# Score matmuls of attention units 4 to 15 issued in eight groups of four instead of twenty smaller groups

## The reference

```python
qkv = x @ attn_qkvw + attn_qkvb                      # (2, 512, 3, 32, 32)
scores = jnp.einsum('bhqd,bhkd->bhqk', q, k) * scale
probs = jax.nn.softmax(scores, axis=-1)
ctx = jnp.einsum('bhqk,bhkd->bhqd', probs, v)
```

## Time and profile before

| | us |
|---|---|
| median of 3 runs | 728.29 |
| lowest and highest | 725.28, 728.97 |
| the profiled execution | 726.08 |
| its span | 724.3 |
| TensorE busy | 705.1 |
| VectorE busy | 472.0 |
| ScalarE busy | 425.9 |

### The profile page before, as it was taken

The page is one execution under the profiler, slowest core; times in us unless marked ns, Lnnn a source line. Parts: engine busy times, 40 slices in busy tenths (PEclk is TensorE's granted clock), DMA queues, the critical chain, the costliest instruction groups (busy, mean ns, idle before and its releaser), DMA issues.

```text
span 724.3 us, 11766 instructions
## 1 busy us (share of the span) xinstructions
PE 705.1 (97%) x3477; PEld 527.6 (73%) x3484; DVE 472.0 (65%) x831; ACT 425.9 (59%) x919; POOL 280.0 (39%) x206
## 2 busy tenths in 40 slices
PE   6999999999999999999999999999999998999996
PEld 5778668668677686686776776857767776888884
DVE  5887567466575584574675755567678798765564
ACT  4458668677686685686766866863655682311111
POOL 5573250170162152143134158735734834211111
PEclk9999999999999999999999999999999999999999
DMA  8667436426436336335444377827733421331101
GB/s 287 177 189 222 115 83 197 122 75 210 109 84 196 92 104 193 92 109 148 134 118 103 92 229 197 257 90 231 249 107 126 155 80 60 129 103 58 59 29 59
DMA packets 55732, 98.97 MB, mean 137 GB/s; under 512 B 10896, under 2 KB 21392, under 8 KB 54800
## 3 DMA queue, kind: packets, MB, share of 16 engines
q1 hardware_dynamic: 55408, 98.13, 44.6%
q10 hardware_dynamic: 288, 0.39, 0.2%
HBM read 56.41 MB, written 16.65 MB: 101 GB/s over the span
## 4 chain that ended last, share of the span: by engine, by line
PE 71%; issue 15%; DVE 6%; POOL 3%; ACT 3%; SPq 1%; DMA 1%; POOLq 0%; DVEq 0%; ACTq 0%
PE bank L469 43%; PE bank L595 8%; PE bank L565 8%; PE bank L609 8%; POOL xb L1205 2%; PE bank L720 1%; PE bank L521 1%; DVE st L1459 1%; DMA w_raw<-in_wqkv 1%; DVE quant L1491 1%; POOL mv L1186 1%; DVE wb_lo L1517 1%; DVE x1s L1506 1%; SPq L232 1%; SPq L227 1%
## 5 line engine op out<-in xcount | busy, mean ns | idle before, releaser
L863 ACT ACTIVATE probs<-bank 128x512 f32<-128x512 f32 x256 | 152.3, 598 | 117.9 <-PE bank L595 115.0
L1385 DVE TENSOR_REDUCE m_col<-bank 128x1 f32<-128x512 f32 x256 | 172.7, 687 | 74.9 <-PE bank L565 74.2
L868 ACT ACTIVATE bank<-bank,m_col 128x512 f32<-128x512 f32 x256 | 169.4, 662 | 19.6 <-DVE m_col L1385 18.0
L469 PE MATMUL bank<-big_hi,w_hi 128*128 128x512 f32 x384 | 157.0, 409 | 5.8 <-DVE big_lo L1280 5.5
L469 PE MATMUL bank<-big_lo,w_hi 128*128 128x512 f32 x384 | 152.7, 398 | 0.0
L469 PE MATMUL bank<-big_hi,w_lo 128*128 128x512 f32 x384 | 151.4, 394 | 0.0
L565 PE MATMUL bank<-kp,qp 96*128 96x512 f32 x256 | 101.5, 397 | 0.7 <-ACT bank L868 0.7
L595 PE MATMUL bank<-qp,kp 98*128 98x512 f32 x256 | 101.0, 398 | 0.0
L469 PEld LDWEIGHTS bank<-big_hi,w_hi 128*128 128x128 f32 x384 | 73.4, 191 | 25.0 <-DVE big_lo L1280 5.9
L469 PEld LDWEIGHTS bank<-big_hi,w_lo 128*128 128x128 f32 x384 | 73.0, 190 | 17.1
L469 PEld LDWEIGHTS bank<-big_lo,w_hi 128*128 128x128 f32 x384 | 73.7, 192 | 14.8
(11 more groups left out here) (139 smaller groups left out, 1106.5 us busy)
## 6 DMA issues: line engine op xcount, KB each, us to landing
w_raw<-in_wqkv SPq DMA_DIRECT2D x7, 1536.0 KB, 7.3
c_raw<-in_ctx SPq DMA_DIRECT2D x16, 512.0 KB, 4.0
qp<-q_hi SPq DMA_DIRECT2D x128, 64.0 KB, 2.0
kp<-k_hi SPq DMA_DIRECT2D x124, 64.0 KB, 2.0
big_raw<-in_xT SPq DMA_DIRECT2D x16, 256.0 KB, 6.0
qp<-q_lo SPq DMA_DIRECT2D x64, 64.0 KB, 2.0
c_scratch<-c_q SPq DMA_DIRECT2D x16, 256.0 KB, 2.2
r_all<-r_scratch SPq DMA_DIRECT2D x64, 64.0 KB, 2.0
```

What stands on the lines that cost most here:

```text
L469: mm = nc.tensor.matmul(dst, lhs[a], rhs[b], start=(k == 0 and n == 0) if first is None else False, stop=(k == last_k and n == 2))
L863: nc.scalar.activation(probs[:, j, t, :], bank(ST0 + i % 2), ACT.Exp).then_inc(sem["exp_ok"], 1)
L868: nc.scalar.activation(bank(max_bank(s, n)), bank(max_bank(s, n)), ACT.Exp, bias=m_col[:, n:n + 1], accum_out=l_col[:, 1 - par, n:n + 1]). ...
L1385: nc.vector.reduce_max(m_col[:, n:n + 1], bank(max_bank(s, n)), AX, negate=True).then_inc(sem["rowmax"], 1)
```

## The change

For steps from 4 on, both slot functions give the same slot for n and n+1 with n even: 2, 7, 12, 18, 23, 29, 34, 40. At such a place S n, T n, S n+1, T n+1 are issued. Only the even ones wait: S n for X n-2, T n for E n-1, which covers the odd ones behind them. On ScalarE the order at a place becomes E n, X n, E n+1, X n+1. Steps 16 and 17 project nothing and keep their order.

```diff
+        def by_pairs(s):
+
+            return not isinstance(s, int) or s >= 4
+
+        def score_slot(n, s):
+
+            if by_pairs(s):
+                return 2 + 38 * (n // 2) // 7
+            return 6 + (34 * n + 14) // 15 if s == 1 else 2 + (38 * n + 14) // 15
+
+        def transposed_slot(n, s):
+
+            if by_pairs(s):
+                return 2 + 38 * (n // 2) // 7
+            return 8 + (39 * n + 14) // 15 if s == 2 else 2 + 3 * n
...
                     if n >= 2 and isinstance(s, int) and s == UNITS:
                         pe.wait_ge(sem["sum_ok"], NS * (s - 1) + n - 1)
+                    elif by_pairs(s) and n >= 2:
+                        if n % 2 == 0:
+                            pe.wait_ge(sem["sum_ok"], NS * (s - 1) + n - 1)
                     elif n >= 3:
...
-                    if n >= 2:
+                    if n >= 2 and not (proj and by_pairs(s)):
                         pe.wait_ge(sem["exp_ok"], NS * (s - 2) + n - 1)
+                    elif n >= 2 and n % 2 == 0:
+                        pe.wait_ge(sem["exp_ok"], NS * (s - 2) + n)
...
-                    if maxima and done < NS and q == score_slot(done, second):
-                        score(done)
-                        done += 1
+                    for _ in range(2):
+                        if maxima and done < NS and q == score_slot(done, s):
+                            score(done)
+                            done += 1
+                        if finish and turned < NS and q == transposed_slot(turned, s):
+                            score_t(turned)
+                            turned += 1
...
-                    if finish and turned < NS and q == transposed_slot(turned, third) + 1:
-                        exp_scores(turned)
-                        turned += 1
-                    if maxima and done < NS and q == (score_slot(done, isinstance(s, int) and s == 1) + 3 if proj else 3 * done + 3):
-                        exp_sum(done)
-                        done += 1
+                    for _ in range(2):
+                        if finish and turned < NS and q == (transposed_slot(turned, s) + 1 if proj else 3 * turned + 3):
+                            exp_scores(turned)
+                            turned += 1
+                        if maxima and done < NS and q == (score_slot(done, s) + (1 if by_pairs(s) else 3) if proj else 3 * done + 3):
+                            exp_sum(done)
+                            done += 1
```

More of the change, by code:

```diff
@@ L658, in step @@
                     return
-                done, turned, third = 0, 0, isinstance(s, int) and s == 2
+                done, turned = 0, 0
                 for q in range(3 * NS):
@@ L665, in step @@
                         project(q // 2)
-                    if maxima and done < NS and q == score_slot(done, second):
-                        score(done)
-                        done += 1
+                    for _ in range(2):
[5 more added lines that the diff above has]
+                            turned += 1
                     if maxima and q == 3 * NS - 3:
                         maxima_to_rows()
-                    if finish and turned < NS and q == transposed_slot(turned, third):
-                        score_t(turned)
-                        turned += 1
                     if finish and q == 6:
```

## The result

| | before | after |
|---|---|---|
| median of the runs on one chip, us | 725.35 (725.28 to 728.97, 5 runs) | 731.93 (731.07 to 732.49, 5 runs) |
| profiled execution, us | 726.08 | 732.25 |
| its span, us | 724.3 | 730.4 |
| steps 4 to 15 of it, us | 343.23 | 349.49 |

The ratio of the runs, after over before, is 1.0076, with a 95% interval of 1.0058 to 1.0094: the change makes the kernel slower by 0.76% (the two medians above alone would give 0.91%, which lies in the interval). The forecast was no change, 727.7 us, and 731.93 lies outside its range of 724.4 to 731.4. It was made from a median of 728.29 for three runs of the kernel before; two more runs brought that median down to 725.35, so the miss is larger than the two times make it look. Of the 6.1 us that the span grew, 6.3 lie in the twelve steps that the change touches, so the rest of the kernel is as it was.

What follows compares the result with a forecast made beforehand. TensorE's matmul pace was taken to bound the kernel. Per step, -0.23 us of pitch and +0.18 of late waits gave -0.05, or -0.6 us over twelve steps: 727.7 us from a median of 728.29, range 724.4 to 731.4.

Steps and rivals of the forecast that it cites:

- The pitch term: TensorE's slow pitches behind scores: 20 places at 0.029 us become 8 at 0.042, gaining 0.23 us a step.
- T2, no loss: Transposed score after a two-slice gap: its load some 0.05 to 0.1 us late, within the free 0.12, costing nothing.
- T12, 0.12: Transposed score whose chain passes R9 behind the clipping: load 0.30 us late, costing 0.12 us a step.
- S to R 0.44: Link from a score on TensorE to its row maximum on VectorE, taken as 0.44 us in the 2.49 us chain.
- VectorE's work and order are unchanged.: Claim that the change leaves what VectorE does and its sequence as they were; no cost was given.
- S n's own wait is no matter: Plain scores' wait for X n-2: claimed done 2.0 us after S n-2, ahead of the 2.31, so no loss.
- T8, 0.06: Transposed score after the two-slice gap from place 3 to 4: chain 0.18 us late, costing 0.06 us a step.
- A late load is cheaper than its lateness, by 0.12: TensorE's weight loads: the second matmul after stands at load + 0.34, so the first 0.12 us is nearly free.
- rival 3: ScalarE's strict order sets the pace, late loads cost in full, no pitch gain: +4.8 us, 733.1; chance 0.08.
- Rival 1: Pitch loss belongs to each score, not each place; only stalls remain: +2.2 us, 730.5; chance 0.17.
- Rival 2: Stalls do not come and the pitch gain stands alone: -2.8 us, 725.5, at best 724.1; chance 0.15.
- Even and odd steps: Sign to watch: a step time differing between even and odd steps would point to something not seen; no size given.

Runs made afterwards that it cites:

- run 5: Changed kernel, each score with its own wait again (S n for X n-3, T n for E n-2), VectorE's packing waits ahead of its projection wait: 724.66 us, ratio 0.9982.
- run 3: Changed kernel with ScalarE's exponentials at a place in the order E, E, X, X instead of E, X, E, X: 731.94 us, ratio 1.0070.
- run 1: Changed kernel with VectorE's four waits on the packing put ahead of its wait on the projection, in both splits: 726.75 us, ratio 1.0005.
- run 6: Changed kernel with four more satisfied packing waits on VectorE ahead of the split of q, from step 4 on: 738.33 us, ratio 1.0171.
- run 7: Kernel before the change with four more satisfied packing waits on VectorE ahead of the split of q: 727.58 us, ratio 1.0031.
- Run 8: The kernel of run 5 with the order S, S, T, T in a group instead of S, T, S, T: 723.84 us, ratio 0.9975.

## Why the prediction was wrong, step by step

- **What bounds the kernel.** Right: TensorE's pace sets it, and only its pitch and a late wait can change the time. Both did.
- **The pitch term,** a gain of 0.23 us a step. Nearly right: 0.19 (28.60 to 28.41, run 5). Both of its halves were a little low, and the errors partly cancel: a group of four costs 0.053 where 0.042 was taken, and with eight of them at 0.42 a gain of 0.19 leaves 0.61 for the 20 places of before, where 0.57 stood.
- **T2, no loss; T12, 0.12.** T2 was right. The late load at T12 came in step 5 alone, where the clipping took 2.38 us; it took 1.71 in step 9, not the 2.11 of the earlier trace rows, and 0.68 in step 8.
- **"S to R 0.44", taken for R6 too.** This is the step that failed. The prediction's chain from S6 to the load of T8 is 2.49 us; measured it is 3.11 (261.23 to 264.34). Its other links came out as taken (R to X 0.71, X to E 0.68, E 0.59, load 0.05), and R6 came 1.08 after S6 instead of 0.44, which is the whole difference. 0.46 of it stood in the trace of before, where R6 comes 0.90 after its score behind the split of q; the other 0.18 is the next item. An estimate from the prediction's own terms with 0.90 for this link: T8 costs 0.18 + 0.46 - 0.12 = 0.52, which covers the 0.30 of T12, and the sum is -0.23 + 0.52 = +0.29 a step, 3.5 us. With 1.08 it is 0.70 at T8 and +0.47 a step, 5.6 us of the 6.26 measured.
- **"VectorE's work and order are unchanged."** The reason for not looking at R6 again, and it does not hold. The instructions and their order are the same, but what hid the waits ahead of the split is not. Before, R5 ran from 257.44 to 258.13, and q's last matmul had started at 256.54; q_hi stood right behind R5 at 258.22, so the waits were run while R5 was at work. After, R5 is over at 259.95, nothing covers the waits, and q_hi comes 1.10 us after q's last matmul. I counted the split as something that lies where it lay, and never asked what R6 would wait for.
- **"S n's own wait is no matter: X n-2 is done 2.0 us after S n-2, ahead of the 2.31."** Wrong in two ways, though in after the late load of T8 covers it. The 2.0 has S to R 0.44, the link of a row maximum that waits only for its score; the one behind the split of q was 0.90 in the very trace of before, and is 1.08 after. And 2.31 is S6 to S8, but a load is due one matmul earlier, at 2.09 (261.23 to 263.32); the prediction had used that rule for T n and forgot it for S n. Measured: 2.62, so 0.53 late.
- **T8, 0.06.** The place was right, the size was not. T8's load came 0.79 late, as E7 waited behind X6, and the place cost 0.66 to 0.77 in steps 4 to 13 and 0.54 to 0.57 in the last two, where 0.06 stood. The twelve steps lost 6.26 us and gained 12 x 0.19 = 2.3 by the pitch, so the stalls are 8.5 us. The place S8, T8 makes up 8.2 of them, and step 5 with its late T12 and T14 the rest.
- **A late load is cheaper than its lateness, by 0.12.** This held: in run 3 S8's load is at 265.61 and T8, the matmul after S8, stands at 265.95, load + 0.34. In after it held for the last late load of the place, T8's at 264.34 with S9 at 264.68, and so it was given once for the two.
- **The count of waits.** Seven waits of each kind were said to go. By the code it is six on the sums (S3 to S15 waited, 13, and 7 stay) and seven on the exponentials, 13 in all. Nothing in the sum hangs on it.
- **The rivals.** The result is rival 3's in size (733.1, at a chance of 0.08) and in its sign of failure, late loads at S. Its mechanism was half right: the row maxima behind which X and E stand set the pace, but at one place only, through VectorE, and with the pitch gain intact. ScalarE's strict order had a part, since E7 stands behind X6 (0.25 of the 0.67, run 3), but its lack of slack was not the cause: run 1 took the loss away without touching ScalarE, and in run 3 S8's load stayed as late. Rival 1 falls by run 5. Rival 2 is what run 5 is: no stalls, 0.19 a step, ratio 0.9982 where it would have had 0.996.
- **Even and odd steps** differ by some 0.1 us (29.17 and 29.07), the sign that I had said would mean something unseen. VectorE's q_hi is 1.21 after q's last matmul in step 8 and 1.10 in step 9. The difference is not new (1.78 and 1.68 in the kernel before, where nobody waited for it), and in steps 14 and 15, which are written out behind the hardware loop, q_hi comes at 1.00 and 0.99. So it goes with the loop, which has an even and an odd half. Why is open.

## What to carry to other kernels

When an order of matmuls is changed and the waits are made coarser, follow every kind of wait back through the engine that feeds it at each place by itself, and take the link from the row at that very place: the maximum behind the split of q came 0.90 after its score where I had taken 0.44 from another place, and that is most of the miss. "The other engine's order is unchanged" is not "its times are unchanged": ask what its waits were hidden behind. And before a saving on waits is made, ask whether they cost anything where they stand; here four satisfied waits on VectorE cost 0.45 us or more a step, and the thirteen removed from TensorE had cost nothing (run 5 has them all and the shortest steps but one).

## What the runs showed of the hardware that I had not expected

- A wait that stands alone (in this kernel with the increment of a counter, `wait_alone`) costs VectorE about 0.11 us even when its semaphore is satisfied: four more of them moved R6 by 0.45 (run 6), and four fewer behind the late one moved q_hi by 0.54 in the loop and by 0.45 in step 14 (run 1).
- TensorE's pitch does not fall back at once to 0.2266 behind matmuls with 96 or 98 rows: the first few behind a group run at 0.231 to 0.240 with nothing waiting, and the order within the group matters a little (0.053 and 0.047 per group).
- The clipping on VectorE, one instruction with one shape, takes 0.68 us when GpSimd runs nothing, as in every even step of all ten kernels. When a GpSimd instruction is under way as the clipping starts, the clipping ends 0.55 us behind that instruction's end (0.55 or 0.56 in every such case where it is lengthened), so it takes up to 2.9 us. In step 9 of after the GpSimd instruction ends at 266.16 and the clipping at 266.71:

```profile
263.78 2.38 POOL L1090 TENSOR_TENSOR w_lo<-w_raw,w_hi 128x1024 fp32r<-128x1024 f32 x1
...
265.00 1.71 DVE L1370 TENSOR_SCALAR c_raw<-c_raw 128x1024 f32<-128x1024 f32 x1
```

  No run moved the GpSimd instruction on purpose; that the clipping is held by it is read from where the two end in the ten traces.
- Step 5 is longer than its neighbours in eight of the ten kernels, by 0.03 us (before) to 0.54 (run 1), and not in runs 7 and 8. In those eight the clipping is under way for 2.3 to 2.9 us in it and R9 comes 2.3 to 3.4 us after S9; in run 7 no GpSimd instruction stands beside it (0.68). Run 8 has R9 as late (3.05) and no late load, and why its order bears that was not followed up.
